# Attention on one core: cosine products as 32-row tiles, a batch's maxima in one trip, one projection copy

## What is computed

```
Q, K, V = x @ Wq + bq, x @ Wk + bk, x @ Wv + bv          # per head
qq, kq = Q @ Wc2q + bc2q, K @ Wc2q + bc2q                # 8 numbers per token and head
fid = (qq . kq) / max(|qq| |kq|, EPS_COS)                # the cosine
qw = fid * (1 + 0.1 * sin(fid * pi))
aw = 0.5 * qw + 0.5 * (Q . K) / sqrt(16)
probs = softmax(aw over keys);  heads = probs @ V
```

## Time and profile before

| | us |
|---|---|
| median of three runs | 512.95 |
| profiled execution, span of its instructions | 513.8 |
| TensorE matmul busy | 385.3 |
| VectorE busy | 368.6 |
| ScalarE busy | 338.0 |
| GpSimd busy | 268.0 |

### The profile page before, as it was taken

The page is one execution under the profiler, slowest core; times in us unless marked ns, Lnnn a source line. Parts: engine busy times, 40 slices in busy tenths (PEclk is TensorE's granted clock), DMA queues, the critical chain, the costliest instruction groups (busy, mean ns, idle before and its releaser), DMA issues.

```text
span 513.8 us, 9151 instructions
## 1 busy us (share of the span) xinstructions
PE 385.3 (75%) x2672; PEld 280.2 (55%) x2672; DVE 368.6 (72%) x891; ACT 338.0 (66%) x713; POOL 268.0 (52%) x406
## 2 busy tenths in 40 slices
PE   1959388979999999999987989460000899999960
PEld 1747155656666666666675346440000688888840
DVE  8586689959999999999965345598860056666670
ACT  1356268959999999999966559532200587778730
POOL 6479044715555555554201041838775047777783
PEclk9997679979999999999999999776555599999995
DMA  9317316456567766776439999001012137666500
GB/s 199 15 36 161 102 48 133 99 111 156 147 157 159 156 154 151 155 152 151 124 61 127 130 124 245 0 11 32 32 54 70 37 85 207 195 186 191 167 14 0
DMA packets 81247, 58.22 MB, mean 113 GB/s; under 512 B 17619, under 2 KB 72919, under 8 KB 81196
## 3 DMA queue, kind: packets, MB, share of 16 engines
q1 hardware_dynamic: 75324, 53.12, 49.4%
q0 software_dynamic: 2496, 4.29, 2.5%
q10 hardware_dynamic: 3376, 0.20, 0.4%
HBM read 35.38 MB, written 23.11 MB: 114 GB/s over the span
## 4 chain that ended last, share of the span: by engine, by line
PE 34%; ACT 28%; DVE 15%; issue 10%; POOL 9%; DMA 2%; SPq 0%; POOLq 0%; DVEq 0%; ACTq 0%
PE ps L1641 9%; PE ps L1652 7%; ACT big L1002 7%; ACT big L1012 6%; POOL sorted_rows L864 3%; ACT L1002 3%; ACT L1012 2%; DVE big L1870 2%; PE ps L1242 2%; PE ps L1543 1%; ACT proj L950 1%; DVE mxs L1847 1%; DVE gb L1718 1%; DVE u_sb L2025 1%; ACT u_turned L957 1%
## 5 line engine op out<-in xcount | busy, mean ns | idle before, releaser
L1847 DVE TENSOR_REDUCE mxs<-ps 128x4 f32<-128x1024 f32 x64 | 75.8, 1221 | 7.3 <-PE ps L1277 4.2
L1870 DVE SCALAR_TENSOR_TENSOR big<-big,ps 128x1024 f32<-128x1024 f32 x64 | 75.0, 1217 | 5.5 <-ACT big L1002 5.2
L1002 ACT ACTIVATE big<-ps 128x1024 f32<-128x1024 f32 x64 | 62.6, 1029 | 8.1 <-PE ps L1413 7.7
L895 POOL DMA_INDIRECT out_dram<-arena,fidx x46 | 46.7, 1015 | 17.9 <-issue 17.6
L2221 DVE TENSOR_SCALAR arena<-ps,x_all 128x128 f32<-128x128 f32 x46 | 14.0, 347 | 56.4 <-PE ps L1661 56.3
L768 POOL CAST mtok<-mxs 128x8 bf16<-128x8 f32 x32 | 6.1, 190 | 82.5 <-DVE mxs L1847 82.5
L1188 ACT ACTIVATE x_all<-x_all 128x128 f32<-128x128 f32 x46 | 20.1, 486 | 44.0 <-DMA x_all<-sorted_rows 44.0
L1641 PE MATMUL ps<-arena,big 128*128 128x256 f32 x184 | 47.2, 403 | 1.1 <-ACT arena L1194 1.1
L1277 PE MATMUL ps<-arena 96*128 96x256 bf16 x256 | 39.5, 293 | 7.3 <-issue 4.6
L1652 PE MATMUL ps<-arena,big 128*128 128x256 f32 x184 | 43.7, 381 | 0.0
L1641 PEld LDWEIGHTS ps<-arena,big 128*128 128x128 f32 x184 | 37.0, 202 | 7.2 <-issue 1.8
(11 more groups left out here) (346 smaller groups left out, 968.3 us busy)
## 6 DMA issues: line engine op xcount, KB each, us to landing
big<-in_L_ffn_w_dram SPq DMA_DIRECT2D x46, 256.0 KB, 3.1
qk_parts<-proj SPq DMA_DIRECT2D x16, 384.0 KB, 2.9
arena<-qk_parts SPq DMA_DIRECT2D x32, 192.0 KB, 3.5
sorted_rows<-zrow SPq DMA_DIRECT2D x16, 266.0 KB, 4.3
arena<-qk_parts SPq DMA_DIRECT2D x32, 128.0 KB, 3.9
proj<-u_parts SPq DMA_DIRECT2D x48, 64.0 KB
x_all<-sorted_rows SPq DMA_DIRECT2D x23, 133.0 KB, 2.5
sorted_rows<-zrow SPq DMA_DIRECT2D x2, 1263.5 KB, 28.3
```

The source lines that it names most:

```text
L895: nc.gpsimd.indirect_dma_start(out2, bass.IndirectOffsetOnAxis(ap=fidx[:, j, t:t + 1], axis=0), fres[j][:, t, :], None, bounds_check=NT * ...
L1002: nc.scalar.activation(W[par][:, n, :], src, ACT.Sin, scale=PI * (1 - 1e-6)).then_inc(sin_ready, 1)
L1847: nc.vector.tensor_reduce(mxs[:, b1 % 2, :, 2 * n:2 * n + 2], src, AX_X, ALU.max, negate=True).then_inc(unit_free, 1)
L1870: nc.vector.scalar_tensor_tensor(W[par][:, n, :], W[par][:, n, :], 10.0, f, ALU.add, ALU.mult).then_inc(unit_free, 1)
```

## The change

Four edits, with the order of the work set anew around them.

The cosine operands of a pair of heads now lie on four groups of 32 partitions, one for each head of four, with two heads on each group one behind the other. A cosine product reads 32 rows at partition 0, 32, 64 or 96, and the products of a unit alternate between two groups. Nothing is filled with zeros, and the memset goes. For this the operands are put twice (four puts of 64 KB) and fetched in two transfers of 128 KB with 1 KB pieces.

A batch's maxima are split, turned, copied, put and fetched once for all eight heads. TensorE turns them before the first logit product of the batch, and that product of the next batch waits for them.

The projections of queries and keys are copied by one ScalarE instruction with the queries' bias for both. The keys' own bias adds the same number to all logits of a query, which the softmax takes out again.

SyncE's order in a batch becomes: put maxima, put cosine operands, fetch maxima, put and fetch queries and keys, fetch cosine operands, zero rows.

```diff
@@ -50,7 +50,8 @@
-    KU = 4 * NQ
+    RG = 4
+    HH = H // RG
@@ -234,8 +235,8 @@
-        u_d = [nc.dram_tensor(f"u_parts{i}", [2, 2, P // 2, S], FP16).ap() for i in range(2)]
-        m_d = [nc.dram_tensor(f"m_parts{i}", [2, H // 2, S], BF16).ap() for i in range(2)]
+        uq_d, uk_d = ([nc.dram_tensor(f"u{n}_parts{i}", [RG, P // 2, S], FP16).ap() for i in range(2)] for n in "qk")
+        m_d = nc.dram_tensor("m_parts", [2, H, S], BF16).ap()
@@ -273,9 +274,7 @@
-        u_st = early(F32, 2 * H * S)
-        uqT, ukT = ([u_st[:, (2 * i + j) * OPW // 2:(2 * i + j + 1) * OPW // 2].bitcast(FP16).rearrange("p (h s) -> p h s", h=H)
-                     for i in range(2)] for j in range(2))
+        uqT, ukT = ([early(FP16, HH, S) for i in range(2)] for j in range(2))
@@ -410,14 +413,15 @@
-        turns = [("u", 0), ("u", 1), ("m0", 0), ("m1", 0)]
+        turns = [("u", 0), ("u", 1), ("m", 0)]
...
-            turns += [(k, b + d) for k, d in (("qk", QK0), ("u", 2), ("m0", 1), ("m1", 1)) if b + d < NB]
+            turns += [(k, b + d) for k, d in (("qk", QK0), ("m", 1), ("u", 2)) if b + d < NB]
...
+        log_order = (1, 0, 3, 2)
@@ -517,10 +521,11 @@
             def put_u(b):
...
-                    sp.wait_ge(u_in[b % 2], 80 * (b // 2))
-                for s in range(2):
-                    sp.dma_start(u_d[b % 2][s].rearrange("j p s -> p j s"),
-                                 u_turned[b % 2][s * P // 2:(s + 1) * P // 2, :, :]).then_inc(u_put[b % 2], 16)
+                    sp.wait_ge(u_in[b % 2], 32 * (b // 2))
+                q, k = (u_turned[b % 2][s * P // 2:(s + 1) * P // 2, :, :] for s in range(2))
+                for a in range(2):
+                    sp.dma_start(uq_d[b % 2][a:RG:2].rearrange("j p s -> p j s"), q).then_inc(u_put[b % 2], 16)
+                    sp.dma_start(uk_d[b % 2][2 * a:2 * a + 2].rearrange("j p s -> p j s"), k).then_inc(u_put[b % 2], 16)
...
             def get_qk(b):
@@ -537,25 +542,22 @@
             def get_u(b):
...
-                sp.wait_ge(u_put[i], 32 * (b // 2 + 1))
+                sp.wait_ge(u_put[i], 64 * (b // 2 + 1))
...
-                q, k = (u_d[i][s].rearrange("j (n h) s -> (j n) h s", h=H) for s in range(2))
-                for lo in (0, 16):
-                    sp.dma_start(uqT[i][lo:lo + 16, :, :], q).then_inc(u_in[i], 16)
-                sp.dma_start(ukT[i][0:16, :, :], k).then_inc(u_in[i], 16)
-                sp.dma_start(ukT[i][16:24, :, :], k[8:16]).then_inc(u_in[i], 16)
-                sp.dma_start(ukT[i][24:32, :, :], k[0:8]).then_inc(u_in[i], 16)
-
-            def put_max(b, r):
-                sp.wait_ge(turn_out, turn_no[f"m{r}", b] + 1)
+                for to, of in ((uqT[i], uq_d[i]), (ukT[i], uk_d[i])):
+                    src = of.rearrange("x (n g c) s -> g (x n) (c s)", g=RG, c=HH)
+                    sp.dma_start(to[:, :, :].rearrange("p c s -> p (c s)"), src).then_inc(u_in[i], 16)
+
+            def put_max(b):
+                sp.wait_ge(turn_out, turn_no["m", b] + 1)
...
-                    sp.wait_ge(m_in[r], 16 * b)
-                sp.dma_start(m_d[r].rearrange("a h s -> (a h) s"), mrow[:, r, :]).then_inc(m_put[r], 16)
-
-            def get_max(b, r):
-                sp.wait_ge(m_put[r], 16 * (b + 1))
-                sp.dma_start(cqT[b % 3][KC:KC + 2, 4 * r:4 * r + 4, :], m_d[r]).then_inc(m_in[r], 16)
+                    sp.wait_ge(m_in, 16 * b)
+                sp.dma_start(m_d.rearrange("a h s -> (a h) s"), mrow[:, :]).then_inc(m_put, 16)
+
+            def get_max(b):
+                sp.wait_ge(m_put, 16 * (b + 1))
+                sp.dma_start(cqT[b % 3][KC:KC + 2, :, :], m_d).then_inc(m_in, 16)
@@ -571,29 +573,24 @@
-            sp.wait_ge(u_zero, 1)
...
-            for r in range(2):
-                put_max(0, r)
-                get_max(0, r)
+            put_max(0)
+            get_max(0)
...
             def body(b, par, first, last, slow):
-                if b + QK0 < NB:
-                    put_qk(b + QK0)
+                if not last:
+                    put_max(b + 1)
...
-                    put_max(b + 1, 0)
-                    put_max(b + 1, 1)
-                    get_max(b + 1, 0)
+                    get_max(b + 1)
...
+                    put_qk(b + QK0)
...
-                if not last:
-                    get_max(b + 1, 1)
@@ -760,14 +757,14 @@
-            def split_max(b, r):
-                pool.wait_ge(unit_free, by_dve[unit_no["max", b, 2 * r + 1]])
+            def split_max(b):
+                pool.wait_ge(unit_free, by_dve[last_of("max", b)])
...
-                    pool.wait_ge(turn_ps, turn_no[f"m{r}", b - 1] + 1)
-                m = mxs[:, b % 2, :, 4 * r:4 * r + 4]
-                nc.gpsimd.tensor_copy(mtok[:, r, :, 0, :], m).then_inc(m_split, 1)
-                pool.wait_ge(m_split, 4 * b + 2 * r + 1)
-                nc.gpsimd.tensor_tensor(mtok[:, r, :, 1, :], m, mtok[:, r, :, 0, :], ALU.subtract).then_inc(m_split, 1)
+                    pool.wait_ge(turn_ps, turn_no["m", b - 1] + 1)
+                m = mxs[:, b % 2, :, :]
+                nc.gpsimd.tensor_copy(mtok[:, :, 0, :], m).then_inc(m_split, 1)
+                pool.wait_ge(m_split, 2 * b + 1)
+                nc.gpsimd.tensor_tensor(mtok[:, :, 1, :], m, mtok[:, :, 0, :], ALU.subtract).then_inc(m_split, 1)
...
             def spread_weights():
@@ -788,11 +785,9 @@
             def body(b, par, first, last, slow):
...
-                    split_max(b + 1, 0)
+                    split_max(b + 1)
...
-                if not last:
-                    split_max(b + 1, 1)
@@ -946,21 +940,20 @@
-                for i in range(2):
-                    q = nc.scalar.activation(qk32[b % 2][:, i, :], bank[:, i * S:(i + 1) * S], ACT.Identity, bias=qk_col[:, i:i + 1])
+                q = nc.scalar.activation(qk32[b % 2].rearrange("p a s -> p (a s)"), bank, ACT.Identity, bias=qk_col[:, 0:1])
...
             def take_u(b):
...
-                    act.wait_ge(u_put[b % 2], 32 * (b // 2))
+                    act.wait_ge(u_put[b % 2], 64 * (b // 2))
...
-            def take_max(b, r):
-                act.wait_ge(turn_ps, turn_no[f"m{r}", b] + 1)
+            def take_max(b):
+                act.wait_ge(turn_ps, turn_no["m", b] + 1)
...
-                    act.wait_ge(m_put[r], 16 * b)
-                nc.scalar.copy(mrow[:, r, :], tb[0:H, 0:S]).then_inc(turn_out, 1)
+                    act.wait_ge(m_put, 16 * b)
+                nc.scalar.copy(mrow[:, :], tb[0:2 * H, 0:S]).then_inc(turn_out, 1)
...
             def roots(hh):
@@ -1027,18 +1019,16 @@
+                if not last:
+                    take_max(b + 1)
...
-                if not last:
-                    take_max(b + 1, 0)
...
-                if not last:
-                    take_max(b + 1, 1)
@@ -1261,11 +1251,11 @@
-            def turn_max(b, r):
-                pe.wait_ge(m_split, 4 * b + 2 * r + 2)
-                bank_free(f"m{r}", b)
+            def turn_max(b):
+                pe.wait_ge(m_split, 2 * b + 2)
+                bank_free("m", b)
...
-                    mm = nc.tensor.transpose(tb[0:H, t * P:(t + 1) * P], mtok[:, r, t, :, :].rearrange("p a h -> p (a h)"), ident_b[:, :])
+                    mm = nc.tensor.transpose(tb[0:2 * H, t * P:(t + 1) * P], mtok[:, t, :, :].rearrange("p a h -> p (a h)"), ident_b[:, :])
...
             def max_unit(b1, n):
@@ -1404,14 +1394,16 @@
                 def cos_unit(n):
...
-                        pe.wait_ge(u_in[par], 80 * (b // 2 + 1))
+                        pe.wait_ge(u_in[par], 32 * (b // 2 + 1))
...
-                    for h in range(2):
-                        for t in range(TPB):
+                    hh = 2 * n // RG
+                    for t in range(TPB):
+                        for h in range(2):
...
-                            mm = nc.tensor.matmul(o[:, c:c + S], of_rows[par][:, 2 * n + h, t * P:(t + 1) * P],
-                                                  of_cols[par][:, 2 * n + h, :], start=True, stop=True)
+                            g = (2 * n + h) % RG * 32
+                            mm = nc.tensor.matmul(o[:, c:c + S], of_rows[par][g:g + 32, hh, t * P:(t + 1) * P],
+                                                  of_cols[par][g:g + 32, hh, :], start=True, stop=True)
@@ -1427,8 +1419,8 @@
-                    if n % 2 == 1:
-                        pe.wait_ge(m_in[n // 2], 16 * (b + 1))
+                    if n == log_order[0]:
+                        pe.wait_ge(m_in, 16 * (b + 1))
@@ -1462,9 +1454,8 @@
-                    turn_max(0, 0)
...
-                    turn_max(0, 1)
+                    turn_max(0)
@@ -1482,6 +1473,8 @@
+                if not last:
+                    turn_max(b + 1)
@@ -1491,13 +1484,9 @@
-                if not last:
-                    turn_max(b + 1, 0)
...
-                if not last:
-                    turn_max(b + 1, 1)
```

(25 more changed lines are left out.)

## The result

The change makes the kernel slower. After it the runs took 533.45 to 540.82 us, median 536.23, beside 514.27 for the kernel before in the same session: a ratio of 1.041, 95% interval 1.036 to 1.046. The forecast was 509.4 us, 503.5 to 517.

A forecast was written before the change was run, and what follows sets the result against it. ScalarE (12.34 of 12.40 us a settled batch) and VectorE (12.19) were taken as full. The terms -5.8 + 0.9 + 2.5 - 0.6 - 0.35 - 0.3 gave -3.65, say -3.6, from 512.95: 509.4 us, range 503.5 to 517.

The forecast's parts named there:

- part 3: Batches 2 to 13: circle through ScalarE's copy, four puts and fetches closes over two batches, period 12.60 us, +2.5 us.
- rival D: Clock at 1.2 GHz through the batches, TensorE binds at 19.8 us a batch, some 600 us; chance 0.03.
- Maxima in one trip: Batch 2's late landing of maxima goes, -5.8 us; TensorE waits for GpSimd's split in batch 1, +0.9 us.
- rival E: In batch 2 the wait for maxima becomes one for queries and keys, about 515 us; chance 0.06.
- ScalarE work: Settled batches: ScalarE falls to 11.8 us, VectorE's 12.2 is the floor, -0.2 us a batch if transfers keep up.
- rival A: Settled batches: transfers keep up and VectorE binds at 12.2 us, 504.5 us in all; chance 0.26.
- Rival B: On SyncE the put of maxima queues behind the last zero rows, circle priced at 13.2 us, 516.5 us; chance 0.17.
- 32-row tiles: Cosine units take between 0.35 and 0.61 us, nothing counted in settled batches, -0.6 us in batch 0.
- Rival C: Tile shape changes at TensorE's cosine products stay uncovered, 0.63 us a batch, 517 us; chance 0.05.
- Zero filling: At the start: without VectorE's memset the statistics begin earlier, -0.35 us at most.
- The last batches: The last two batches, without query and key traffic, keep the shorter ScalarE work, -0.3 us.

The follow-up runs named there:

- e1: The changed kernel with the put of query and key parts first in a batch on SyncE; 514.72 us, ratio 0.9978.
- e6: e1 with full products, the zero filling and the two puts and five fetches of the kernel before; 508.23 us, ratio 0.9855.
- e2: The changed kernel with the zero rows of every batch moved behind the last batch; period 12.95 us, one execution of 528.98 us.
- e7: e1 with queries, keys and maxima moved before the cosine operands of batch 1 on SyncE, ahead of the first batch; 513.17 us, ratio 0.9938.
- e8: e6 with queries, keys and maxima moved before the cosine operands of batch 1 on SyncE, ahead of the first batch; 507.98 us, ratio 0.9852.

## Why the prediction was wrong

The step that failed is part 3, SyncE's order: the right circle, with both of its halves too small, and a second circle that I treated as its rival and that runs beside it. The settled period was 13.66 us where I said 12.60, and no rival but D, with its 600 us, reached the 536 us.

1. *Maxima in one trip*: right. Batch 2 fell by 5.3 us (forecast 5.8), with a stop of 1.42 us for query and key transfers left in it, a smaller rival E; the new wait ahead of batch 1's logits was 0.78 us (forecast 0.9). It lies in the row of batch 0 in the table.

```profile
90.74 0.38 PE L1258 MATMUL ps<-ident_b,mtok 128*16 128x128 bf16 x2 [0.78 <-POOL mtok L767]
...
105.11 1.09 PE L1420 MATMUL ps<-ident,big 128*128 128x128 f32 x8 [0.23 <-DVE big L1858]
...
118.06 1.09 PE L1420 MATMUL ps<-ident,big 128*128 128x128 f32 x8 [0.20 <-DVE big L1858]
```

2. *ScalarE work*: the direction was right, the floor was not. I took VectorE's busy 12.19 us as the floor of a batch; with transfers that keep up (e1, e6) it is 11.97, so rival A was priced 12 x 0.23 = 2.8 us too high.

3. *SyncE's order*: from the end of the copy to the next M I counted 12.23 us; the chain shows 203.33 - 189.99 = 13.34. The put of the parts took 3.74 and not 2.9 us, and the fetch of the maxima 0.55 and not 0.35. What stretched that put I can't say: the one at 166.86, also behind four puts, landed in 2.76, and there this half took 12.67. Back from M to the copy's end I counted 12.2 + 0.76 = 12.96; it took 189.99 - 175.99 = 14.00, and 14.25 in the pair before. This half has the clock in it, which was low behind the wait (0.63 from 175.9 to 179.4 us): from M to the first cosine products TensorE took 5.27 us, and 3.93 in the next batch, without a wait.

```profile
175.99 1.16 PE L1267 MATMUL ps<-arena 96*128 96x256 bf16 x8 [1.76 <-DMA arena<-qk_parts]
...
181.26 0.90 PE L1405 MATMUL ps<-proj 32*128 32x256 f16 x8
...
189.26 1.03 PE L1267 MATMUL ps<-arena 96*128 96x256 bf16 x8 [0.16 <-DVE big L1888]
...
193.19 0.90 PE L1405 MATMUL ps<-proj 32*128 32x256 f16 x8
```

 So the pair is 27.34 in place of 25.19, 13.67 a batch where I said 12.60, and 12 x 1.07 = 12.8 us are missing from the sum for this alone; the other 9 us between the forecast's -3.6 and the profile's +17.9 lie in the batches and stages at both ends (parts 4 to 6). Rival B's circle came out at 13.21 us, as I priced it (13.2), but in part by luck: the zero rows were issued 3.9 us after the first fetch and not 5.0, and landed 5.84 us later and not 4.9 + 0.3. The mistake was to set it against the forecast, at a chance of 0.17: the chain that ended last goes through one circle in some batches and through the other in others, so neither excludes the other.

 In rival D I thought of a clock that is low all the time or not at all. In the settled batches after the change it was low for 3 to 4 us behind each of the five stops of 1.8 to 2.6 us, which turns a late transfer into a later copy and feeds the circle. Not every such stop did this: e6's of 2.35 us in batch 2 was followed by rows at 1.00, and so was one of 2.24 us in e2, at 187.53, with tiles.

```profile
104.00:110.00 6.00, 5.68 (x46) 4.74 (x47) 5.01 (x6) 4.15 (x5) 0.28 (x2) 1.00 0.68 170
```

4. *32-row tiles*: in settled batches as forecast. A unit of four cosine products takes 0.39 us in place of 0.61, within the bounds, and gives nothing, since TensorE doesn't bind; e1 and e6 have nearly the same period. In the first batches the sign was wrong: with one order (e1 against e6) the tiles cost 3.5 us ahead of batch 0, 1.6 in it and 1.5 in batch 1, in place of -0.6. The products did get shorter, but the first maxima landed later, behind the tiles' own puts and 1 KB fetches, and the clock stayed low for longer. Rival C's gaps stayed covered.

```profile
183.15 0.39 PE L1405 MATMUL ps<-proj 32*128 32x256 f16 x4
```

5. *Zero filling*: the 0.35 us are not to be seen; the first transposes came 1.2 us later.

6. *The last batches*: +1.4 us in batch 14 and 2.5 behind it, forecast -0.3. Batch 14 is 1.4 to 4.3 us longer in all kernels of the table and in e7 and e8, with tiles or without (e6: 19.0 us, clock 0.67 from 250 to 260 where before shows 1.00). Why the clock falls there I did not find, nor what the 2 us behind the batches are: e8, which has e6's code there, took 241.8 us for that part, less than the kernel before, so they may belong to the execution and not to the change.

Taken apart: with the old place for the put of parts and full products the rest of the change (maxima in one trip, one projection copy and their order, not tested one by one) is worth -1.5%; the tiles take 1.2% back with that order, and the late put takes 4.4% with tiles.

## What to carry to other kernels

Where one engine issues all transfers, its order is a schedule: a wait in it holds back everything behind it, and the sign of too late an issue was here that the issuing engine never waited for the data it sends. Put the transfer that closes the longest circle first, behind nothing that waits, and write each circle out in full with every instruction that it passes; when two circles come out within a few per cent of each other, expect both, now the one and now the other, and allow for a low clock behind a stop. An edit that shortens work on an engine that doesn't bind (the tiles) can still cost by the transfers that it needs.

## What the runs showed of the hardware

- After the change a stop of TensorE of 1.77 us before a batch's products was followed by 3.9 us at 0.56 of the full clock, in a stretch in which it was busy 3.83 us. In e6 a stop of 2.35 us was followed by 6 us at 1.00, so the length of the stop alone doesn't say it.
- Four 32-row products that alternate between two groups took 0.39 us, against 0.61 for four full ones, 1.6 times. The Trainium skill (TensorE: Matmul & The Clock Gate, Part 3) gives 3.07 for four tiles on four groups; no run here had four groups at once.
- A put of 384 KB landed 3.8 us after its issue behind fetches in 4 KB pieces (kernel before, ahead of batch 0) and 5.9 to 6.4 us after it behind a fetch of like size in 1 KB pieces (e1 and after), where twice as many puts of 64 KB stood ahead too. Zero rows right behind such fetches took a median of 5.7 us to land where they took 4.3. The Trainium skill (Perfetto Trace Analysis, DMA Optimizations) says that small transfers, under 2 KB, have significant overhead each; read of the pieces of a transfer, the trace agrees.
